# Local transformer on one core: Newton's step moves to GpSimd, and the orders of all engines change with it

## The reference

```python
for i in range(DEPTH):                                   # 6
    x = attn_layer(shift_tokens(x), Wqkv[i], q_scale[i], k_scale[i], Wo[i]) + x
    x = ffn_layer(shift_tokens(x), ln_g[i], ln_b[i], W1[i], b1[i], W2[i], b2[i]) + x

def attn_layer(x, Wqkv, qs, ksc, Wo):                    # 16 heads of 64
    q, k, v = jnp.split(x @ Wqkv, 3, -1)
    q = l2norm(q) * qs;  k = l2norm(k) * ksc             # x / max(||x||, 1e-12)
    q = q * cos * scale + rotate_half(q) * sin * scale
    k = k * cos / scale + rotate_half(k) * sin / scale
    out = local_attention(q, k, v)                       # windows of 32, this one and the last
    return out @ Wo
def ffn_layer(x, g, bln, W1, b1, W2, b2):
    a, gate = jnp.split((layernorm(x) * g + bln) @ W1 + b1, 2, -1)
    return a * gelu(gate) @ W2 + b2
```

## Time and profile before

| | us |
|---|---|
| median of 3 runs | 4414.74 |
| profiled execution, its own time | 4419.39 |
| its span (first to last instruction) | 4417.6 |
| mean granted TensorE clock | 0.940 |

### The profile page before, as it was taken

The page is one execution under the profiler, slowest core; times in us unless marked ns, Lnnn a source line. Parts: engine busy times, 40 slices in busy tenths (PEclk is TensorE's granted clock), DMA queues, the critical chain, the costliest instruction groups (busy, mean ns, idle before and its releaser), DMA issues. The chain is left out here.

```text
span 4417.6 us, 164417 instructions
## 1 busy us (share of the span) xinstructions
PE 3899.8 (88%) x64144; PEld 2853.1 (65%) x64144; DVE 3447.6 (78%) x6675; ACT 3176.4 (72%) x10347; POOL 2673.5 (61%) x2507
## 2 busy tenths in 40 slices
PE   7966968999999999999954896899999999999996
PEld 3423437777777777777734664777777777777773
DVE  1132129999999999999943664999999999999994
ACT  3343337888888888888841433788888888888884
POOL 1110127777777777777710332777777777877772
PEclk8987989999999999999975987999999999999997
...
GB/s 58 57 15 44 57 47 105 115 103 119 100 116 103 106 112 108 114 97 109 117 29 0 1 0 33 103 112 104 119 99 116 104 108 112 103 117 98 106 119 37
DMA packets 549303, 377.81 MB, mean 86 GB/s; under 512 B 32576, under 2 KB 533056, under 8 KB 546240
## 3 DMA queue, kind: packets, MB, share of 16 engines
...
## 5 line engine op out<-in xcount | busy, mean ns | idle before, releaser
L1266 POOL TENSOR_TENSOR lt_t<-lt_t 128x512 f32<-128x512 f32 x768 | 973.5, 1289 | 567.8 <-DVE lt_t L1100 567.8
L1002 ACT ACTIVATE lt_pb<-lt_pb,lt_mx 128x64 f32<-128x64 f32 x3072 | 1023.5, 346 | 0.0
L1272 POOL TENSOR_TENSOR lt_t<-lt_t,lt_rn 128x512 f32<-128x512 f32 x768 | 810.8, 1076 | 118.4 <-DVE lt_rn L1128 117.1
L49 PE MATMUL ps<-lt_wh,lt_xh 128*128 128x512 f32 (+1 forms) x1536 | 581.8, 379 | 148.9 <-DVE lt_t L1100 87.6
L1002 ACT ACTIVATION_READ_ACCUMULATOR lt_pb<-lt_pb,lt_mx 128x1 f32 x3072 | 610.2, 199 | 0.0
L984 ACT ACTIVATE lt_qkT<-ps 128x512 f32<-128x512 f32 x768 | 459.0, 598 | 197.2 <-PE ps L804 196.8
L1111 DVE TENSOR_REDUCE lt_ss<-lt_sq 128x8 f32<-128x512 f32 x768 | 518.7, 675 | 14.5 <-ACT lt_sq L979 9.9
L1100 DVE TENSOR_TENSOR lt_t<-ps,lt_tab 128x512 f32<-128x512 f32 x768 | 522.9, 681 | 2.9
L51 PE MATMUL ps<-lt_wh,lt_xl 128*128 128x512 f32 (+1 forms) x1536 | 523.7, 341 | 0.0
L1106 DVE TENSOR_TENSOR lt_t<-ps,lt_tab 128x512 f32<-128x512 f32 x768 | 521.6, 679 | 1.6 <-PE ps L804 0.3
L50 PE MATMUL ps<-lt_wl,lt_xh 128*128 128x512 f32 (+1 forms) x1536 | 522.8, 340 | 0.0
...
## 6 DMA issues: line engine op xcount, KB each, us to landing
lt_vw<-v_scratch SPq DMA_DIRECT2D x768, 256.0 KB, 3.7
...
```

Of the source, the lines that this page charges most:

```text
L49: nc.tensor.matmul(out, lh, rh, start=start, stop=False)
L1002: ins = nc.scalar.activation(p, p, ACT.Exp, bias=mx[:, par, c:c + 1], accum_out=sm[:, par, c:c + 1])
L1266: nc.gpsimd.tensor_tensor(o, o, t2[:, t, :], ALU.add).then_inc(padd[t], 1)
L1272: nc.gpsimd.tensor_tensor(o, o, rn[:, u[1] % 2, 8 * t:8 * t + 8].unsqueeze(2).to_broadcast([P, 8, DH]), ALU.mult).then_inc(qkd[t], 1)
```

## The change

It does the following, all of it in `local_transformer_phase`.

- `newton` goes from DVE (three operations, 128x16 each) to GpSimd (four: square, times v, minus 3 by a constant tile `three`, times y0), each waiting for the one before.
- DVE: `lengths` and `floor` work on u1 in place of u0, `take_values` on u2 in place of u1, `inverse_sums` on u4 in place of u3. `first_guess` on ACT, `values` on PE and the store and loads of the values on SP follow one unit later too, and so does `normalise_weights` on GpSimd.
- `turn` and `take_turned` of half 0 stand at the end of the slot of u1; those of half 1 come in the slot after, as u2. `turn_weights` and `take_weights` come one slot later and stand near the head of the slot.
- `next_batch`, which copies and splits the next sequence's input, runs in a sequence's third unit, not its second.
- All four orders are new. `gelus` stands between the two halves of `exponentials`; the third gate product stands behind `merge`; the second and third `product` run at offsets 20 and 21, not 18 and 22. The casts of Wqkv stay last in the slots of ACT and GpSimd.

The diff, without the memory and initial values of the tile `three`, one offset on SP (the reload of `fvl` at s = 14, not 15) and the left-most 16 blanks of each line:

```diff
@@ -771,12 +771,12 @@
         load_columns(sp, w2, "lt_w2", layer, 0, w2ld)

 def slot(L, s):
-    u1 = unit(L, s - 1)
+    u2 = unit(L, s - 2)
     if not isinstance(L, int) or L < DEPTH:
         reload(L, s)
-    if u1:
-        spread(u1)
-stream(sp, slot, 1)
+    if u2:
+        spread(u2)
+stream(sp, slot, 2)
 for j in range(GJ):
     sp.wait_ge(wrld[j], 16 * (DEPTH + 1))

@@ -797,7 +797,9 @@
 def turn(u, t):
     upto(pe, qkd[t], u)
     if t == 0:
-        upto(pe, vE, u)
+        upto(pe, vE, back(u, 1))
+        if unit(u[0], u[1] - 1) is None:
+            upto(pe, tE[1], back(u, 1))
     else:
         upto(pe, tE[0], u)
     for q in range(4):
@@ -806,7 +808,7 @@

 def values(u):
     j, half = u[1] % GJ, batch(u) % 2
-    upto(pe, tE[1], back(u, 1))
+    upto(pe, tE[1], u)
     c = slice(j * GROUPCOLS + 512, (j + 1) * GROUPCOLS)
     for t in range(2):
         ins = exact_product(nc, V_[:, t * HG * DH:(t + 1) * HG * DH],
@@ -883,7 +885,7 @@
     nc.tensor.matmul(two(F_[:, :]), avg[:, :], xs(c), start=True, stop=True).then_inc(fmean, 1)

 def variance(c):
-    upto_pair(pe, fdev, c, 1, 1)
+    upto_pair(pe, fhd, pair(c[0], c[1] - 1), 3, 3)
     upto_pair(pe, fsq, c)
     nc.tensor.matmul(F_[:, :], avg[:, :], sqf[:, :], start=True, stop=True).then_inc(fvar, 1)

@@ -909,13 +911,13 @@
     elif k == 1:
         upto_pair(pe, fhd, c, 1, 3)
     else:
-        upto_pair(pe, flog, pair(c[0], c[1] + 1), 1, 1)
+        upto_pair(pe, fdev, pair(c[0], c[1] + 1), 1, 1)
         if pair(c[0], c[1] + 1) is None:
             upto_pair(pe, fhd, c, 2, 3)
     exact_product(nc, F_[0:n, :], (w1h[:, o:o + n], w1l[:, o:o + n]), (rh[:, :], rl[:, :])).then_inc(fa, 1)

 def down(c):
-    upto_pair(pe, fhd, c, 3, 3)
+    upto_pair(pe, flog, pair(c[0], c[1] + 1), 1, 1)
     if c[1] == 0:
         pe.wait_ge(w2ld, c[0] * 16 + 16)
     upto_pair(pe, fhd, c, 3, 3)
@@ -924,51 +926,50 @@
     ins.then_inc(fy, 1)

 def slot(L, s):
-    u0, u1, u2, u4, u5 = unit(L, s), unit(L, s - 1), unit(L, s - 2), unit(L, s - 4), unit(L, s - 5)
-    c = chunk(L, s, 17)
-    if c:
-        gate(c, 1)
+    u0, u1, u2, u5 = unit(L, s), unit(L, s - 1), unit(L, s - 2), unit(L, s - 5)
+    c = chunk(L, s, 23)
+    if c:
+        down(c)
+    if u5:
+        turn_weights(u5)
+    c = chunk(L, s, 18)
+    if c:
+        linear(c, 0)
     c = chunk(L, s, 13)
     if c:
         mean(c)
     if u0:
         project(u0, 0)
         project(u0, 1)
-    c = chunk(L, s, 17)
-    if c:
-        gate(c, 2)
-    c = chunk(L, s, 23)
-    if c:
-        down(c)
+    c = chunk(L, s, 18)
+    if c:
+        linear(c, 1)
     if u2:
-        turn(u2, 0)
-    c = chunk(L, s, 17)
-    if c:
-        linear(c, 0)
-    c = chunk(L, s, 18)
-    if c:
-        linear(c, 1)
+        turn(u2, 1)
     if u5:
         weigh(u5)
+    c = chunk(L, s, 17)
+    if c:
+        gate(c, 1)
+    c = chunk(L, s, 17)
+    if c:
+        gate(c, 0)
+    c = chunk(L, s, 21)
+    if c:
+        linear(c, 2)
     c = chunk(L, s, 14)
     if c:
         variance(c)
     if u2:
-        turn(u2, 1)
-    if u4:
-        turn_weights(u4)
+        values(u2)
+        scores(u2)
     if u5:
         merge(u5)
-    if u2:
-        scores(u2)
-    c = chunk(L, s, 16)
-    if c:
-        gate(c, 0)
+    c = chunk(L, s, 17)
+    if c:
+        gate(c, 2)
     if u1:
-        values(u1)
-    c = chunk(L, s, 22)
-    if c:
-        linear(c, 2)
+        turn(u1, 0)
 stream(pe, slot, 16)

 @block.scalar
@@ -1033,45 +1034,46 @@
     if c[1] == 0:
         act.wait_ge(fvgld, c[0] * 16 + 16)
     for k, (o, n) in enumerate(DB):
-        upto_pair(act, fg, c, (1, 2, 3)[k], 3)
+        upto_pair(act, fg, c, (2, 1, 3)[k], 3)
         upto_pair(act, fhd, pair(c[0], c[1] - 1), k + 1, 3)
         into = PT_ if k == 1 else F_
         nc.scalar.activation(gl[0:n, k, :], into[0:n, :], ACT.Gelu, bias=fvg[0:n, k:k + 1]).then_inc(fgd, 1)
     nc.scalar.preload_act_table_set("natural_log_exp_and_others")

 def slot(L, s):
-    u0, u2, u3, u4, u5 = unit(L, s), unit(L, s - 2), unit(L, s - 3), unit(L, s - 4), unit(L, s - 5)
-    c = chunk(L, s, 16)
-    if c:
-        high(c)
-    c = chunk(L, s, 17)
-    if c:
-        gelus(c)
+    u0, u1, u2, u3, u5 = unit(L, s), unit(L, s - 1), unit(L, s - 2), unit(L, s - 3), unit(L, s - 5)
     if s == 15 and running(L):
         high_up(act, L)
+    if u5:
+        take_weights(u5)
+    c = chunk(L, s, 16)
+    if c:
+        high(c)
+    c = chunk(L, s, 14)
+    if c:
+        square_deviation(c)
     if u0:
         square_of(u0, 0)
-    c = chunk(L, s, 14)
-    if c:
-        square_deviation(c)
+    if u1:
+        first_guess(u1)
     if u2:
-        take_turned(u2, 0)
+        take_turned(u2, 1)
     if u0:
         square_of(u0, 1)
     if u5:
         take_output(u5)
-    if u2:
-        take_turned(u2, 1)
     c = chunk(L, s, 14)
     if c:
         inverse_deviation(c)
-    if u4:
-        take_weights(u4)
     if u3:
         exponentials(u3, 0)
+    c = chunk(L, s, 17)
+    if c:
+        gelus(c)
+    if u3:
         exponentials(u3, 1)
-    if u0:
-        first_guess(u0)
+    if u1:
+        take_turned(u1, 0)
     if next_layer(L, s, 30, 0) is not None:
         high_group(act, next_layer(L, s, 30, 0), 0)
     if next_layer(L, s, 30, 1) is not None:
@@ -1114,19 +1116,8 @@
 def floor(u):
     upto(dve, ssd[0], u)
     upto(dve, ssd[1], u)
+    upto(dve, rnd, back(u, 2))
     nc.vector.tensor_tensor(vm[:, u[1] % 2, :], ss[:, u[1] % 2, :], res["tiny"][:, :], ALU.max).then_inc(vmd, 1)
-
-def newton(u):
-    par = u[1] % 2
-    upto(dve, y0d, u)
-    nc.vector.tensor_tensor(ya[:, par, :], y0[:, par, :], y0[:, par, :], ALU.mult).then_inc(newt, 1)
-    upto(dve, newt, u, 1, 2)
-    nc.vector.tensor_tensor(yb[:, par, :], ya[:, par, :], vm[:, par, :], ALU.mult).then_inc(newt, 1)
-    upto(dve, newt, u, 2, 2)
-    upto(dve, qkd[0], back(u, 2))
-    upto(dve, qkd[1], back(u, 2))
-    nc.vector.scalar_tensor_tensor(out=rn[:, par, :], in0=yb[:, par, :], scalar=-3.0, in1=y0[:, par, :],
-                                   op0=ALU.add, op1=ALU.mult).then_inc(rnd, 1)

 def mask_scores(u):
     upto(dve, simd, u)
@@ -1190,46 +1181,47 @@
                                            in1=x, op0=ALU.add, op1=ALU.add).then_inc(fx, 1)

 def slot(L, s):
-    u0, u1, u2, u3, u5 = unit(L, s), unit(L, s - 1), unit(L, s - 2), unit(L, s - 3), unit(L, s - 5)
+    u0, u1, u2, u3, u4, u5 = unit(L, s), unit(L, s - 1), unit(L, s - 2), unit(L, s - 3), unit(L, s - 4), unit(L, s - 5)
+    c = chunk(L, s, 18)
+    if c:
+        product(c, 0)
+    if u1:
+        lengths(u1, 0)
+    c = chunk(L, s, 13)
+    if c:
+        deviation(c)
+    c = chunk(L, s, 15)
+    if c:
+        normalise(c)
+    if u1:
+        lengths(u1, 1)
+    if u4:
+        inverse_sums(u4)
+    if u1:
+        floor(u1)
+    c = chunk(L, s, 20)
+    if c:
+        product(c, 1)
     if u3:
         maxima(u3)
-    if u1:
-        newton(u1)
-    c = chunk(L, s, 17)
-    if c:
-        product(c, 0)
-    c = chunk(L, s, 15)
-    if c:
-        normalise(c)
+    c = chunk(L, s, 23)
+    if c:
+        update(c)
     if u0:
-        lengths(u0, 0)
         cosine(u0, 0)
-        lengths(u0, 1)
+        sine(u0, 0)
+    if u2:
+        take_values(u2)
+    if u0:
+        cosine(u0, 1)
         sine(u0, 1)
-        floor(u0)
+    c = chunk(L, s, 21)
+    if c:
+        product(c, 2)
     if u5 and u5[1] % GJ == GJ - 1:
         update_x(u5)
-    if u0:
-        sine(u0, 0)
-        cosine(u0, 1)
-    c = chunk(L, s, 18)
-    if c:
-        product(c, 1)
-    if u1:
-        take_values(u1)
-    c = chunk(L, s, 22)
-    if c:
-        product(c, 2)
     if u2:
         mask_scores(u2)
-    c = chunk(L, s, 13)
-    if c:
-        deviation(c)
-    if u3:
-        inverse_sums(u3)
-    c = chunk(L, s, 23)
-    if c:
-        update(c)
 dve.wait_ge(fvlld, 16)
 stream(dve, slot, 16)

@@ -1247,11 +1239,11 @@
                             ALU.subtract).then_inc(xsd, 1)

 def next_batch(u):
-    if u[1] % GJ == 1:
-        n = unit(u[0], u[1] - 1 + GJ)
+    if u[1] % GJ == 2:
+        n = unit(u[0], u[1] - 2 + GJ)
         if n is None:
             return
-        read, c = level(pool, back(u, 2)), pair(n[0] - 1, n[1] // UP)
+        read, c = level(pool, back(u, 3)), pair(n[0] - 1, n[1] // UP)
         ready = c and level_pair(pool, c)
         pool.wait_ge(xsd, 1)
         if read is not None:
@@ -1265,6 +1257,17 @@
     o = t1[:, u[1] % 2, t, :]
     nc.gpsimd.tensor_tensor(o, o, t2[:, t, :], ALU.add).then_inc(padd[t], 1)

+def newton(u):
+    par = u[1] % 2
+    upto(pool, y0d, u)
+    nc.gpsimd.tensor_tensor(ya[:, par, :], y0[:, par, :], y0[:, par, :], ALU.mult).then_inc(newt, 1)
+    upto(pool, newt, u, 1, 3)
+    nc.gpsimd.tensor_tensor(yb[:, par, :], ya[:, par, :], vm[:, par, :], ALU.mult).then_inc(newt, 1)
+    upto(pool, newt, u, 2, 3)
+    nc.gpsimd.tensor_tensor(ya[:, par, :], yb[:, par, :], res["three"][:, :], ALU.subtract).then_inc(newt, 1)
```

(43 more changed lines are left out.)

28 lines of the change are left out of this document (15 added, 13 removed).

## The result

The changed kernel takes 4576.03 us (median of 4 runs, 4572.48 to 4582.58) beside 4414.97 for the kernel before (4410.19 to 4417.79) on the same chip. The ratio is 1.0362, 95% interval 1.0347 to 1.0378: 161 us slower, where I forecast 65. The profiled execution has a span of 4570.7 us.

A forecast was written before the change was run, and what follows sets the result against it. DVE (97% busy) sets the pace, PE (95%) close behind. A layer: 4 x 64.4 + 12.3 + 0.9 = 270.8 against 264.0 us; +82 over twelve, -12 and -5 for phase ends, together +65: 4480 us, range 4365 to 4560.

The forecast's parts named there:

- the price of Newton: Newton's four small operations on GpSimd: 1.2 us a unit, about 0.22 us each plus some 0.08 before the next.
- `floor` being held: DVE's `floor` waits until GpSimd's `add_turned` ends, delaying ACT's copy; slot 6 loses 0.45 us.
- DVE under 85%: Sign expected in the trace after the change: DVE's busy share under 85%, from 97% in the earlier window.
- rival 1: PE catches up: lead between engines swallows gaps in slots 0 to 2; 61.5 us a pair, 4340 us, chance 0.25.
- rival 2: The casts cost little: the chain at the layer boundary closes loosely, 5 us not 12.3; 4400 us, chance 0.10.
- The new floor of PE: PE's back-to-back work in a pair of eight units, summed from single products: 60.4 us.
- The pair walked through: Eight slots without casts, walked in each engine's order with waits beyond PE's sum: 64.4 us a pair.
- The casts: Weight casts in a closed ACT, GpSimd, PE chain: 12.3 us a layer boundary, 0.9 more for `high_up` and `low_up`.
- PE catches up: Lead carried from slot to slot swallows gaps in slots 0 to 2: 61.5 us a pair, 4340 us, chance 0.25.
- The casts cost little: ACT's cast is done before GpSimd gets there: boundary 5 us not 12.3, 4400 us, chance 0.10.
- GpSimd becomes the bound: Newton at 0.5 us an operation on GpSimd, 64.3 us a pair, every wait on it grows: 4550 us, chance 0.10.

The follow-up runs named there:

- e2: The changed kernel with the casts of layers after the first cut to 16 of 768 columns: 4458.32 us, ratio 1.0101.
- e3: The kernel before with the casts of layers after the first cut to 16 of 768 columns: 4369.19 us, ratio 0.9901.
- e13: The changed kernel with merge(u5) ahead of scores(u2) and the casts of later layers cut to 16 of 768 columns: 4387.51 us, ratio 0.9940.
- e9: The changed kernel with merge(u5) ahead of scores(u2) instead of behind it: 4514.98 us, ratio 1.0239.
- e10: The changed kernel with unread transposes in PE's gaps ahead of turn(u2, 1) at the casts: 4547.13 us, ratio 1.0316.
- e4: The kernel before with only Newton moved to GpSimd, four operations ahead of normalise_qk(u1, 0), all orders kept: 4337.42 us, ratio 0.9822.
- e5: The changed kernel, all new orders kept, with Newton back on DVE in three operations: 4580.26 us, ratio 1.0361.
- e11: The changed kernel with GpSimd's part of the casts behind the next slot's normalise_qk(u2, 1), and merge ahead of scores: 4431.61 us, ratio 1.0044.
- e15: The kernel before with Newton alone on GpSimd and the casts of later layers cut to 16 of 768 columns: 4304.52 us.

## Why the prediction was wrong

Right were the direction, the price of Newton (1.2 us forecast, 1.19 measured), `floor` being held (405 ns on average, 243 in the earlier trace rows), DVE under 85%, and the casts as the place of PE's waits for `normalise_qk`. Two numbers of the text are slips without effect: the eight exponentials take 2.68 us by their rows, not 2.66, and rival 1 with a third of rival 2 is 0.28, not 0.27. The size was wrong, and e2, e3 and e13 say where. Windows of e3, e2 and e13, in this order:

```profile
3000.00:4200.00 1200.00, 1154.02 (x23676) 905.70 (x23675) 1157.91 (x2334) 1052.85 (x3753) 925.14 (x894) 1.00 0.38 112
```

```profile
3000.00:4200.00 1200.00, 1125.43 (x22825) 895.14 (x22824) 1007.36 (x1827) 1026.75 (x3622) 1002.89 (x1440) 0.99 0.40 107
```

```profile
3000.00:4200.00 1200.00, 1141.81 (x23360) 898.32 (x23358) 1033.70 (x1867) 1051.91 (x3703) 1030.35 (x1474) 1.00 0.41 110
```

Without the length of the casts a pair takes 64.8 us before (e3), 67.0 in the new orders (e2) and 65.6 with most of the stops gone (e13); layer lengths by `low`, over four.

1. **The new floor of PE**, "a pair: 60.4 us". Mis-sized. PE's busy share gives 1141.81/1200 x 65.6 = 62.4 a pair in e13 and 1154.02/1200 x 64.8 = 62.3 in e3. The figure was in my own rows: 1136.81/1200 x 66.0 = 62.5. I did that sum for DVE and ACT and built PE's from single products instead, and came out 2.0 too low.
2. **The pair walked through**, 64.4. The 4.0 us of waits that I laid on that floor were too many (3.2 in e13, all idle time counted); with the right floor they would have made 66.4. Of what was missing besides, the stops inside `scores` are 1.4 a pair (67.0 to 65.6), 71 us in all by e2 and e13, 61 by e9. The sum had no term for them; in the kernel before PE stops there for 1.0 us between 800 and 2000 us. So ordinary pairs, forecast at 64.4 where e3 measures 64.8 for the kernel before, lost 89 us.
3. **The casts**, 12.3 + 0.9 a boundary. Right in the mechanism and near in size: their length costs 10.7 measured, 4.1 before. The waits of PE into slots 7, 0, 1 and 2 were forecast as 1.1, 3.0, 3.1 and 2.6 us and are 1.19, 2.48, 2.48 and 3.81 in the boundary above: nearly the same sum, divided otherwise. The loop with gelus and table loads took 15.7 us between two turns, where I had 12.2 (9.6 and 2.6), so I had the greatest loss one slot too early. Part of all this is the clock, up to 29 us by e10, which I hadn't counted.
4. **The rivals.** *PE catches up*: refuted, and excluded from the start by point 1, since 61.5 a pair lies below PE's own work. *The casts cost little*: refuted by e2. *GpSimd becomes the bound*: its condition, 0.5 us an operation, is refuted by the 0.22 above; e4, where GpSimd runs at 90% in a faster kernel, and e5, where freeing it changes nothing, speak against it too.

The step that failed is thus the walked pair of 64.4 us. A layer took 278.6 us where I had 270.8, and 7.8 over twelve layers is 94 of the 96 us by which the forecast fell short. Four pairs at 67.0 in place of 64.4 are 10.4 of it: 5.6 from the stops, 4.8 from the floor of PE less the idle time counted too high. What is left of the layer for the casts, 10.6 against 13.2, takes 2.6 back.

The loss itself divides into 73 (casts), 71 (stops, e2 to e13) and 18 (rest of the orders, e13 against e3). That these give the whole 161 is no proof of them, since they are differences in one chain of times; that casts and stops are separate rests on e11. The last 18 contain Newton's gain. Against e15, which has the same Newton and the small casts in the old orders, e13 is 83 us slower (4387.5 to 4304.5): that much the new orders give away besides stops and casts. It stays open which of their many moves does that.
